# Windows of edges packed over groups of sixteen tiles in place of eight

## The chip, the cores and the metric

The kernel runs on one core of a Trainium2 chip. Its time is the time on the device, in microseconds, and the time of a version is the median of its runs. The core has five engines with instruction streams of their own: PE (TensorE, matrix products; PEld is its loading of weights), DVE (VectorE), ACT (ScalarE), POOL (GpSimd) and SP (SyncE). They meet at semaphores only. Transfers run on 16 DMA engines; the gathers of this kernel are issued by GpSimd.

## The reference

There are 50,000 nodes with 128 features and 100,000 directed edges: 25,000 random pairs, each in both directions, and one loop for each node, sorted by their end `dst`. Cut to what matters (`sage` three times, then one layer of attention):

```
h = relu(layernorm(x))
for l in range(3):                       # Wl, Wr, b of layer l
    agg = segment_sum(h[src], dst) / max(deg, 1)
    h = leaky_relu(agg @ Wl.T + b + h @ Wr.T, 0.01)
x = x + h
h = relu(layernorm(x)) @ W
e = leaky_relu(h[src] @ att_src + h[dst] @ att_dst, 0.2)
e = exp(e - segment_max(e, dst)[dst])
alpha = e / (segment_sum(e, dst)[dst] + 1e-16)
out = x + segment_sum(h[src] * alpha[:, None], dst) + bias
```

## The kernel before

**Tiles and passes.** The nodes are cut into 196 tiles of 256 (`NG`, `TILE`), each of two halves of 128. The program has a preparation and four passes over the tiles: passes 1 to 3 are the three layers (the third also does the sum with x, the second norm and `h @ W`), pass 4 is the attention. In a pass every engine goes through the tiles in one written order, `steps`, and at step t it works on tile t, or on one some steps behind.

**Windows.** The sums over edges are matrix products. A window is a list of up to 128 edges: `idx` has a column with their sources and `dcol` one with their ends. GpSimd gathers the 128 source rows of a window from the node table by one indirect DMA (L635), into one of 27 slots of `rows`. VectorE compares a row of numbers with the column of `dcol`, which gives a mask of 128 edges x 256 nodes (L1247; in pass 4 a bf16 form, L1249). TensorE multiplies rows by mask (L852, three matmuls a tile). Loops are not in the windows, a tile adds its own rows by itself.

**Lists.** A half tile has about 128 edges, some more and some fewer, so edges are packed over a group of `WG` = 8 tiles: its list has `GW` = 2 x 8 + 1 = 17 windows for 16 halves. Window k takes what half k - 1 has left over, and then edges of half k; the last takes only what is left. So a tile touches three windows, and shares two of them with its neighbours, except at the border of a group. The first tile of a group issues three gathers and each other one two (`s.new` in the code). There are 25 groups, and the last one has four tiles and 9 windows: 24 x 17 + 9 = 417 windows a pass. At the border the first and the last window of a group concern one half only, and `columns` gives their masks 128 columns in place of 256.

**Surplus.** `lead` is what a half finds left over from the halves before it in its group; it must not pass 128 at any window. If it does, `flag` is 0 and all engines take a general branch, which goes through the edges in 782 blocks of 128, each with an indirect load and an indirect store.

**How the surplus is found.** The preparation runs on 98 partitions (`HALF`), one for two tiles; a group of 8 tiles is `GROUP_ROWS` = 4 partitions. Each partition works out its surplus as if none came in, its total, and writes them to `carry`. TensorE moves `carry` down by 1, 2 and 3 partitions (L823, with the shifted unit matrices of `shift_m`, which GpSimd makes at L558). VectorE copies the result to `prev` and goes from the furthest partition to the nearest, three operations for each (L1110 to L1112); `later` (L1012) is 1 where the partition k before belongs to the same group. The helper `op` makes each operation of VectorE here wait for the one before it. Further on, the columns of `idx` and `dcol` are copied from PSUM, one copy for each partition of a group (L1178), and one for the last window of the groups (L1180).

**What lies around it.** Between these pieces VectorE does the statistics of the first norm for the 49 blocks of four tiles (`groups(a, b)`, L1034 to L1048), and ScalarE the norm itself (L662, L669). The node table is stored when the norm is done; the gathers of pass 1 wait for that.

**What orders a pass.** GpSimd issues gathers in order; before those of tile t it waits for the products of tile t - 12 to be done (`agg_done`, in pass 4 `pv_done`). TensorE waits at tile t for the masks and rows of it. In pass 4 ScalarE adds a score to each mask (L782), TensorE turns it (L953), VectorE takes the maximum (L1450).

Of the kernel before, what the change touches and what calls it, by code (L numbers as in the profile page):

```python
# [7 lines left out]
ALU = mybir.AluOpType  # L8
# [13 lines left out]
SG = 4  # L22
NSG = NG // SG
SW = 2 * SG + 1
WG = 8
GW = 2 * WG + 1
GROUPS = -(-NG // WG)
LAST_W = 2 * (NG - (GROUPS - 1) * WG) + 1
NWIN = (GROUPS - 1) * GW + LAST_W
GROUP_ROWS = WG // 2  # L30
RUN = 5 * P
# [8 lines left out]
HALF = NG // 2  # L40
# [22 lines left out]
class Step:  # L63


    def __init__(self, i, off):
# [12 lines left out]
        self.k = off % SG  # L79
        self.m = off % WG  # L80
        own = off // WG * GW + 2 * self.m
        self.w = own if i is None else WRING * i + own
# [86 lines left out]
def build(nc, x, src, dst, wl1, bl1, wr1, wlh, blh, wrh, w_gat, att_s, att_d, bias, out):  # L169
# [11 lines left out]
    with ctx:  # L181
        def sb(name, shape, dt=F32):
            return ctx.enter_context(nc.sbuf_tensor(name, shape, dt))
# [87 lines left out]
        nth_i = sb("nth_i", [HALF, 1], I32)  # L271
        later = sb("later", [HALF, GROUP_ROWS])
        came = sb("came", [HALF, 2])
        prev = sb("prev", [HALF, 9])
        carry = sb("carry", [HALF, 3])
        shift_m = sb("shift_m", [HALF, GROUP_ROWS - 1, HALF])
        stat = sb("stat", [P, 8])
# [79 lines left out]
        bank = [ctx.enter_context(nc.psum_tensor(f"bank{i}", [P, 512], F32)) for i in range(8)]  # L357
# [627 lines left out]
        def vector_program(eng):  # L985
# [9 lines left out]
            def op(ins):  # L995

                seq[0] += 1
                ins.then_inc(S["prep_seq"], 1)
                eng.wait_ge(S["prep_seq"], seq[0])
# [103 lines left out]
                                        ALU.mult, ALU.add))  # L1103
            op(eng.tensor_tensor(word[:, :, :], w_a[:, :, :], valid[:, :, :], ALU.mult))
            eng.wait_ge(S["chain_ps"], 1)
            op(eng.tensor_copy(prev[:, :], bank[1][0:HALF, 3:12]))
            op(eng.tensor_tensor(came[:, 0:1], prev[:, 6:7], later[:, 3:4], ALU.mult))
            for k in (2, 1):
                to = came[:, 0:1] if k > 1 else lead[:, 0:1]
                op(eng.tensor_tensor(came[:, 1:2], prev[:, 3 * k - 2:3 * k - 1], came[:, 0:1], ALU.add))  # L1110
                op(eng.tensor_tensor(came[:, 1:2], came[:, 1:2], prev[:, 3 * k - 3:3 * k - 2], ALU.max))
                op(eng.tensor_tensor(to, came[:, 1:2], later[:, k:k + 1], ALU.mult))  # L1112
# [685 lines left out]
        block.scalar(scalar_program)  # L1798
        block.tensor(tensor_program)
        block.vector(vector_program)  # L1800

_INS = ['x', 'src', 'dst', 'L0_gnn_Wl1', 'L0_gnn_bl1', 'L0_gnn_Wr1', 'L0_gnn_Wlh', 'L0_gnn_blh', 'L0_gnn_Wrh',
# [18 lines left out]
```

## Time and profile before

| | |
|---|---|
| median of 3 runs | 2512.96 us (2511.53 to 2515.49) |
| span of the profiled execution | 2514.0 us (its own time is not listed beside its span) |
| busy PE, DVE, ACT, POOL | 74%, 79%, 55%, 66% |
| gathers by L635 | 1251 in passes 1 to 3, 417 in pass 4 |
| DMA | 582.84 MB, 232 GB/s in the mean |
| preparation, to the first gather | 232.86 us |

The profile is one execution. A share of busy time is a mean over stages with different limits, so the stages are read apart: by the busy time in a stretch of time, by the rows of single instructions, and by the waits. The time in brackets at an instruction is the idle time of its engine before it and what ended it; "issue" means that nothing in the profile did.

### The profile page before, as it was taken

The page shows a single profiled execution, that of the slowest core. Times are in us where ns is not written, and L with a number is a line of the kernel's source. Part 1 is how long each engine was busy: PE and PEld are TensorE (multiplying, and loading weights), DVE is VectorE, ACT ScalarE, POOL GpSimd, SP SyncE. Part 2 cuts the span into 40 slices and gives each one's busy share as a digit, 9 for nine tenths or more (in the row PEclk, how much of TensorE's full clock was granted, in tenths as well). Part 3 has the DMA queues.
Part 4 walks back from the last instruction along what each step waited for, and adds up shares of the span by engine and source line. Part 5 has one row for each costly group of instructions (what it writes and reads, how often), then busy time and mean ns, then how long its engine had stood idle before and what let it go on. Part 6 is the DMA issues. An engine that isn't in the chain of part 4 may idle for free. (4 is left out here: it accounts for less than half of the span.)

```text
span 2514.0 us, 49419 instructions
## 1 busy us (share of the span) xinstructions
PE 1865.3 (74%) x12376; PEld 1627.8 (65%) x12376; DVE 1991.2 (79%) x8222; ACT 1393.8 (55%) x3711; POOL 1648.2 (66%) x1706
## 2 busy tenths in 40 slices
PE   0000888888886887888887999999999566666666
PEld 0000777777775777777766888888888456555555
DVE  7988766666664666666656999999999699999999
ACT  3696344444442222222223666666666688888887
POOL 2002777777775777777766777767672577777774
PEclk9999999999998999999998999999999799999998
DMA  6685788888886888888886988888888588887887
GB/s 207 216 296 204 235 249 245 247 249 246 249 248 180 244 253 244 244 251 242 251 231 200 264 263 261 258 256 255 257 256 234 139 205 204 206 202 202 205 203 174
DMA packets 597881, 582.84 MB, mean 232 GB/s; under 512 B 79531, under 2 KB 557349, under 8 KB 597568
## 3 DMA queue, kind: packets, MB, share of 16 engines
q1 hardware_dynamic: 402272, 337.58, 44.7%
q0 software_dynamic: 54208, 112.76, 21.0%
q10 hardware_dynamic: 141120, 129.32, 15.0%
q8 instruction: 107, 1.75, 0.3%
q14 instruction: 174, 1.43, 0.2%
HBM read 372.40 MB, written 207.75 MB: 231 GB/s over the span
## 5 line engine op out<-in xcount | busy, mean ns | idle before, releaser
L635 POOL DMA_INDIRECT rows<-tab,idx x1251 | 1229.4, 983 | 548.7 <-issue 342.6
L852 PE MATMUL bank<-mask,rows 128*128 128x128 f32 (+1 forms) x3528 | 645.6, 320 | 208.9 <-DMA rows<-tab,idx 185.9
L852 PEld LDWEIGHTS bank<-mask,rows 128*128 128x128 f32 x3528 | 543.9, 195 | 286.4 <-issue 165.6
L1267 DVE TENSOR_TENSOR sage<-bank,sage 128x256 f32<-128x256 f32 x588 | 247.2, 420 | 413.2 <-PE bank L852 410.9
L722 ACT ACTIVATE sage<-bank,b_col 128x256 f32<-128x256 f32 x392 | 185.9, 474 | 599.6 <-PE bank L878 599.1
L635 POOL DMA_INDIRECT rows<-tab_c,idx x417 | 398.1, 955 | 181.5 <-issue 115.8
L1247 DVE TENSOR_SCALAR mask<-iota,dcol 128x256 f32<-128x256 f32 (+1 forms) x1251 | 418.8, 365 | 0.1
L953 PE MATMUL bank<-ident,mask 128*128 128x128 f32 x784 | 139.9, 305 | 177.5 <-ACT mask L782 176.8
L1273 DVE TENSOR_TENSOR sage<-sage 128x256 f32<-128x256 f32 x588 | 246.3, 419 | 1.8 <-DMA sage<-inv_d 1.6
L1278 DVE SCALAR_TENSOR_TENSOR sage<-sage 128x256 f32<-128x256 f32 x588 | 243.0, 413 | 4.6 <-ACT sage L722 4.6
L877 PE MATMUL bank<-sage,wcat 128*128 128x256 f32 x784 | 236.9, 384 | 0.0
L878 PE MATMUL bank<-sage,wcat 128*128 128x256 f32 x784 | 236.0, 383 | 0.0
L953 PEld LDWEIGHTS bank<-ident,mask 128*128 128x128 f32 x784 | 90.8, 151 | 208.1 <-ACT mask L782 195.2
L963 PE MATMUL bank<-rows,sage 128*128 128x131 f32 x1568 | 224.3, 290 | 1.4 <-ACT sage L802 1.4
L782 ACT ACTIVATE mask<-cut_w,rows 128x256 f32<-128x256 bf16 (+1 forms) x417 | 181.0, 484 | 61.1 <-issue 39.0
L963 PEld LDWEIGHTS bank<-rows,sage 128*128 128x128 f32 x1568 | 207.6, 205 | 1.6 <-ACT sage L802 1.6
L691 ACT ACTIVATE sage<-sage,nmr,rstd 128x128 f32<-128x128 f32 x392 | 172.2, 486 | 42.9 <-DVE nmr L1224 41.6
L802 ACT ACTIVATE sage<-cut_w,ed 128x256 f32<-128x256 bf16 (+1 forms) x441 | 184.4, 473 | 4.9 <-DVE ed L1475 2.6
L917 PE MATMUL bank<-wcat,sage 128*128 128x128 f32 x784 | 177.3, 308 | 0.0
L886 PEld LDWEIGHTS bank<-ident,sage 128*128 128x128 f32 x784 | 152.9, 196 | 22.8 <-issue 4.9
L878 PEld LDWEIGHTS bank<-sage,wcat 128*128 128x128 f32 x784 | 150.9, 192 | 20.9
L1450 DVE TENSOR_REDUCE mx<-bank 128x2 f32<-128x512 f32 x196 | 132.7, 677 | 33.8 <-PE bank L953 33.4
(219 smaller groups left out, 3276.9 us busy)
## 6 DMA issues: line engine op xcount, KB each, us to landing
sage<-inv_d SPq DMA_DIRECT2D x588, 128.0 KB
turned<-sage ACTq DMA_DIRECT2D x392, 128.0 KB
tab<-sage ACTq DMA_DIRECT2D x392, 128.0 KB
sage<-turned SPq DMA_DIRECT2D x392, 128.0 KB
tab_c<-sage ACTq DMA_DIRECT2D x196, 132.0 KB
own_w<-tab_c SPq DMA_DIRECT2D x196, 132.0 KB, 2.9
tab<-sage SPq DMA_DIRECT2D x49, 512.0 KB, 3.5
xin<-tab SPq DMA_DIRECT2D x196, 128.0 KB
```

The costliest lines, as they stand in the source:

```text
L635: eng.indirect_dma_start(out=rows[:, s.win[w], 0:width], out_offset=None, in_=table, in_offset=bass.IndirectOffsetOnAxis(ap=idx[:, s.w + w ...
L722: eng.activation(new_t[:, o.v, :], ps_zz[ph][o.t % len(ps_zz[ph])][:, 0:TILE], ACT.Identity, bias=b_col[:, ph - 1:ph]).then_inc(S["z_a"], 1)
L802: m = eng.activation(prob[:, o.mw[w], a:b], cut[:, o.win[w], a:b], ACT.Exp, bias=ed[:, o.g, 2 * o.k + w:2 * o.k + w + 1])
L852: m = eng.matmul(to[:, a:b], rows[:, s.win[w], 0:D], mask[:, s.mw[w], c:c + b - a], start=(w == 1), stop=(w == 2))
L877: eng.matmul(to, wcat[:, ph - 1, D:2 * D], own_t[:, o.v, :], start=True, stop=False)
L878: eng.matmul(to, wcat[:, ph - 1, 0:D], agg_t[:, o.r, :], start=False, stop=True).then_inc(S["dense_done"], 1)
L953: m = eng.transpose(ps_z[s.t % 3][:, j * TILE + n * P:j * TILE + (n + 1) * P], score[:, s.mw[j + n], (1 - n) * P:(2 - n) * P], ident[:, :])
L963: m = eng.matmul(ps_o[o.k][:, j * TILE:j * TILE + D + 3], prob[:, o.mw[j + n], (1 - n) * P:(2 - n) * P], rows[:, o.win[j + n], 0:D + 3], s ...
L1247: m = eng.tensor_scalar(to[:, g.mw[w], a:b], io[:, a:b], node, None, ALU.is_equal)
L1267: eng.tensor_tensor(agg_t[:, o.r, :], ps[:, 0:TILE], own_t[:, o.v, :], ALU.add).then_inc(S["sum_v"], 1)
L1273: eng.tensor_tensor(agg_t[:, o.r, :], agg_t[:, o.r, :], inv_b[:, o.r, :], ALU.mult).then_inc(S["t_v"], 1)
L1278: eng.scalar_tensor_tensor(at, at, 0.01, at, ALU.mult, ALU.max).then_inc(S["l_v"], 1)
```

## The change

`WG` becomes 16. A group is then 16 tiles or 8 partitions, a list 33 windows for 32 halves, and there are 13 groups, the last one again with four tiles and 9 windows: 12 x 33 + 9 = 405 windows. The surplus is carried over 32 halves, and a partition takes it from the seven before it. `GW`, `GROUPS`, `LAST_W`, `NWIN`, `GROUP_ROWS` and the sizes of `later` and `shift_m` follow from `WG`. Behind the new line all line numbers are higher by one.

```diff
--- before.py
+++ after.py
@@ -22,7 +22,7 @@
 SG = 4
 NSG = NG // SG
 SW = 2 * SG + 1
-WG = 8
+WG = 16
 GW = 2 * WG + 1
 GROUPS = -(-NG // WG)
 LAST_W = 2 * (NG - (GROUPS - 1) * WG) + 1
@@ -271,7 +271,7 @@
         nth_i = sb("nth_i", [HALF, 1], I32)
         later = sb("later", [HALF, GROUP_ROWS])
         came = sb("came", [HALF, 2])
-        prev = sb("prev", [HALF, 9])
+        prev = sb("prev", [HALF, 3 * (GROUP_ROWS - 1)])
         carry = sb("carry", [HALF, 3])
         shift_m = sb("shift_m", [HALF, GROUP_ROWS - 1, HALF])
         stat = sb("stat", [P, 8])
@@ -1103,9 +1103,10 @@
                                         ALU.mult, ALU.add))
             op(eng.tensor_tensor(word[:, :, :], w_a[:, :, :], valid[:, :, :], ALU.mult))
             eng.wait_ge(S["chain_ps"], 1)
-            op(eng.tensor_copy(prev[:, :], bank[1][0:HALF, 3:12]))
-            op(eng.tensor_tensor(came[:, 0:1], prev[:, 6:7], later[:, 3:4], ALU.mult))
-            for k in (2, 1):
+            op(eng.tensor_copy(prev[:, :], bank[1][0:HALF, 3:3 * GROUP_ROWS]))
+            far = GROUP_ROWS - 1
+            op(eng.tensor_tensor(came[:, 0:1], prev[:, 3 * far - 3:3 * far - 2], later[:, far:far + 1], ALU.mult))
+            for k in range(far - 1, 0, -1):
                 to = came[:, 0:1] if k > 1 else lead[:, 0:1]
                 op(eng.tensor_tensor(came[:, 1:2], prev[:, 3 * k - 2:3 * k - 1], came[:, 0:1], ALU.add))
                 op(eng.tensor_tensor(came[:, 1:2], came[:, 1:2], prev[:, 3 * k - 3:3 * k - 2], ALU.max))
```

On VectorE, in the preparation, where the surplus of the partitions before is added up (before, then after; `came` is the surplus that comes in):

```order
L1106 COPY prev<-bank 98x9
L1107 TENSOR_TENSOR came<-prev,later 98x1
L1110 TENSOR_TENSOR came<-prev,came 98x1
L1111 TENSOR_TENSOR came<-came,prev 98x1
L1112 TENSOR_TENSOR came<-came,later 98x1
L1110 TENSOR_TENSOR came<-prev,came 98x1
L1111 TENSOR_TENSOR came<-came,prev 98x1
L1112 TENSOR_TENSOR lead<-came,later 98x1
```

```order
L1106 COPY prev<-bank 98x21
L1108 TENSOR_TENSOR came<-prev,later 98x1
L1111 TENSOR_TENSOR came<-prev,came 98x1
L1112 TENSOR_TENSOR came<-came,prev 98x1
L1113 TENSOR_TENSOR came<-came,later 98x1
```

The last three rows stand six times in a row now, the last time with `lead` as what is written. So there are 12 more operations between the copy of `prev` and the windows' places.

On GpSimd, the gathers of passes 1 to 3 and of pass 4 (as a difference):

```order
 L606 ISA x2
 L607 COMPARE_AND_BRANCH
-L635 DMA rows<-tab,idx 128x128 x1251
-L635 DMA rows<-tab_c,idx 128x132 x417
+L635 DMA rows<-tab,idx 128x128 x1215
+L635 DMA rows<-tab_c,idx 128x132 x405
 L607 UNCONDITIONAL_BRANCH
```

There are 36 gathers fewer in the first three passes and 12 in the fourth. The copies of L1178 into `idx` and `dcol`, four each before, of 96 or 100 columns, are eight each now, of 48 or 52 columns.

On VectorE in pass 1, at the border behind the eighth tile (before, then after; `mask` is what the window's comparison writes):

```order
L1247 TENSOR_SCALAR mask<-iota,dcol 128x256
L1247 TENSOR_SCALAR mask<-iota,dcol 128x128
L1273 TENSOR_TENSOR sage<-sage 128x256
L1267 TENSOR_TENSOR sage<-bank,sage 128x256
L1247 TENSOR_SCALAR mask<-iota,dcol 128x128
L1247 TENSOR_SCALAR mask<-iota,dcol 128x256 x2
```

```order
L1248 TENSOR_SCALAR mask<-iota,dcol 128x256 x2
L1274 TENSOR_TENSOR sage<-sage 128x256
L1279 SCALAR_TENSOR_TENSOR sage<-sage 128x256
L1268 TENSOR_TENSOR sage<-bank,sage 128x256
L1248 TENSOR_SCALAR mask<-iota,dcol 128x256 x2
```

The two half masks, one at the end of a group and one at the start of the next, have become one whole mask that both tiles share.

## Rows read from the trace of the kernel before

**Rows 1.** Busy time (instructions) of PE, PEld, DVE, ACT, POOL; clock, DMA share, GB/s.

```profile
161.00:229.00 68.00, 0.00 (x0) 0.00 (x0) 52.70 (x348) 68.00 (x188) 0.00 (x0) 1.00 0.82 285
233.00:768.00 535.00, 449.90 (x2690) 397.47 (x2691) 345.79 (x1013) 219.30 (x572) 408.12 (x417) 1.00 0.82 239
785.00:1313.00 528.00, 422.49 (x2300) 369.22 (x2301) 325.11 (x985) 141.56 (x376) 400.88 (x417) 0.96 0.84 242
1400.00:1900.00 500.00, 497.70 (x3350) 423.34 (x3348) 486.69 (x2091) 317.41 (x958) 358.35 (x354) 1.00 0.89 258
1990.00:2490.00 500.00, 328.72 (x2985) 296.55 (x2986) 482.92 (x2452) 440.59 (x1051) 379.01 (x398) 0.94 0.81 201
```

**Rows 2.** Timeline of POOL: start, duration, instruction [idle before].

```profile
232.86 1.00 POOL L635 DMA_INDIRECT rows<-tab,idx  x1 [100.06 <-DMA tab<-sage]
...
767.29 0.94 POOL L635 DMA_INDIRECT rows<-tab,idx  x1 [0.30 <-issue]
785.04 0.94 POOL L635 DMA_INDIRECT rows<-tab,idx  x1 [16.81 <-DMA tab<-sage]
...
1311.76 0.94 POOL L635 DMA_INDIRECT rows<-tab,idx  x1 [0.30 <-issue]
...
1965.61 0.94 POOL L635 DMA_INDIRECT rows<-tab_c,idx  x1 [54.76 <-DMA tab_c<-sage]
...
2489.55 0.94 POOL L635 DMA_INDIRECT rows<-tab_c,idx  x1 [0.30 <-issue]
```

**Rows 3.** Waits of POOL in passes 3 and 4: us, times, longest.

```profile
POOL rows L635 <- PE bank L852: 58.5, 90, 0.9
...
POOL rows L635 <- PE bank L963: 11.0, 36, 0.3
```

**Rows 4.** Waits of PE in passes 1 and 2, of DVE in 1990:2490.

```profile
PE bank L852 <- DMA rows<-tab,idx: 62.4, 79, 1.9
...
PE bank L852 <- DMA rows<-tab,idx: 107.4, 97, 10.7
...
DVE mx L1450 <- PE bank L953: 11.3, 19, 1.7
```

**Rows 5.** Groups by form: count | busy, mean ns of one | idle before.

```profile
L635 POOL DMA_INDIRECT rows<-tab,idx x1251 | 1229.4, 983 | 548.7 <-issue 342.6 <-DMA tab<-sage 134.1 <-PE bank L852 71.9
...
L635 POOL DMA_INDIRECT rows<-tab_c,idx x417 | 398.1, 955 | 181.5 <-issue 115.8 <-DMA tab_c<-sage 54.8 <-PE bank L963 11.0
L1247 DVE TENSOR_SCALAR mask<-iota,dcol 128x256 f32<-128x256 f32 x1101 | 383.5, 375 | 0.0
...
L1249 DVE TENSOR_SCALAR cut_w<-iota_b,dcol 128x256 bf16<-128x256 bf16 x367 | 94.6, 290 | 0.0
L1247 DVE TENSOR_SCALAR mask<-iota,dcol 128x128 f32<-128x128 f32 x150 | 44.3, 295 | 0.1
...
L1249 DVE TENSOR_SCALAR cut_w<-iota_b,dcol 128x128 bf16<-128x128 bf16 x50 | 15.1, 303 | 0.0
```

**Rows 6.** Timeline of DVE and ACT in the preparation.

```profile
73.06 0.16 DVE L1110 TENSOR_TENSOR came<-prev,came 98x1 f32<-98x1 f32 x1
...
74.03 0.16 DVE L1112 TENSOR_TENSOR lead<-came,later 98x1 f32<-98x1 f32 x1
...
154.89 1.14 DVE L1178 TENSOR_SCALAR idx<-bank 128x100 int32<-128x100 f32 x4
156.06 0.20 DVE L1180 TENSOR_SCALAR idx<-bank 128x24 int32<-128x24 f32 x1
...
160.82 0.30 ACT L662 ACTIVATE std<-mv,eps 128x8 f32<-128x8 f32 x1 [0.84 <-DVE mv L1039]
```

**Rows 7.** Waits in the preparation; a DMA issue: count, us to landing.

```profile
POOL row_d L579 <- DVEq L1027: 5.1, 1, 5.1
...
PE bank L826 <- DVEq L1125: 11.0, 1, 11.0
...
head<-packed,slice_i POOLq DMA_INDIRECT x5, 3.5
```

## The prediction

> **What bounds the kernel now.** I read the cut into stages first, then the issue rows of GpSimd's gathers, then who waits for whom in each stage. The program has a preparation (0 to 233 us) and four passes over the 196 tiles. [rows 1] give, for each pass, the busy time of the engines, and no engine looks full in passes 1 and 2: TensorE is busy 449.9 of 535 us and 422.5 of 528 us, VectorE less, GpSimd 408.1 and 400.9. In the steady part of pass 3 TensorE is busy 497.7 of 500 us. In pass 4 VectorE is busy 482.9 of 500 us and GpSimd 379.0.
>
> Busy time misleads for GpSimd. [rows 2] are its issue rows: a gather takes 0.94 us, and 0.30 us of idle time stand before the next, put down to "issue". So a gather costs 1.25 us, and 0.94 of it counts as busy. By the starts of the first and last of 417, pass 1 issues them from 232.86 to 767.29 us (1.285 us each, some slow ones at its start among them), pass 2 from 785.04 to 1311.76 (1.266), pass 4 from 1965.61 to 2489.55 (1.259). [rows 3] say that in pass 4 GpSimd never waits for a free buffer: the longest wait on TensorE is 0.3 us, which is the gap that is there anyway (36 cases; passes 1 and 2 have the same row with 23 and 21). In pass 3 it is otherwise: 90 waits, 58.5 us, the longest 0.9; there GpSimd is held back. The other side agrees. [rows 4]: in passes 1 and 2 TensorE waits 79 and 97 times for gathered rows (62.4 and 107.4 us), and in the steady part of pass 3 it is full [rows 1]. So passes 1 and 2 are paced by the number of gathers, pass 3 by TensorE, and pass 4 by gathers with VectorE close behind: there VectorE waits 19 times for scores from TensorE, 11.3 us in all in 500.
>
> The preparation is a chain on two engines. ScalarE waits for VectorE a last time before 160.82 us [rows 6]; from 161 to 229 us it is busy 68.00 of 68 us [rows 1], and the first gather follows at 232.86 [rows 2].
>
> **The change part by part.**
>
> *Gathers.* A list of windows now covers 16 tiles with 33 windows in place of 2 x 17 = 34. With 13 lists in place of 25 there are 12 x 33 + 9 = 405 windows in place of 417: 12 gathers fewer in each pass, 1215 and 405 in place of the counts of [rows 5].
> - Passes 1 and 2: 12 x 1.266 = 15.2 us each, by the mean of pass 2, since the slow gathers at the start of pass 1 stay. The next limit in these passes is TensorE: 422.5 busy of 528, so a pass of 513 us leaves it 90 idle. DMA engines are busy 0.84 of pass 2 at 242 GB/s, and 0.89 at 258 GB/s in pass 3 [rows 1], so the denser traffic has been carried. Bounds: 9 to 16 us for each.
> - Pass 3: TensorE's matmuls are the same in number and shape (three for each tile), and it is full. 0 us, at most the 2.6 us that VectorE saves there.
> - Pass 4: 12 x 1.259 = 15.1 us if GpSimd alone decides. But VectorE is nearly as late: 482.9 busy of 500. What it can give back is the 11.3 us that it waits for scores [rows 4] and its own saving of 3.8 us (below), together 15.1, and to get all of it no gap could be left. At the low end only the 3.8 comes. I take 12 us, nearer to the upper end, since the waits are there now and late rows are what makes them.
>
> *Masks.* At each of the 12 list borders that go, two half masks (128 columns) become one whole mask (256). Pass by pass on VectorE: 2 x 295 - 375 = 215 ns, 12 times: 2.6 us; in pass 4 with the bf16 form, 2 x 303 - 290 = 316 ns, 12 times: 3.8 us [rows 5]. In passes 1 and 2 this lies beside VectorE's waits for TensorE and is worth nothing. ScalarE's score activations shrink in the same way in pass 4, where it is not the bound (440.6 of 500).
>
> *Carrying the surplus over seven rows.* Here the change adds. Each operation of the preparation waits for the one before it, so an operation costs the distance of two starts: from 73.06 to 74.03 us there are five, 0.195 us each [rows 6].
> - Four more comparisons for `later`: 0.8 us, ahead of the load of `row_d`, for which GpSimd waits 5.1 us on VectorE [rows 7]; they shift that load.
> - Four more turns of three operations: 12 x 0.195 = 2.3 us.
> - The copies into `idx` and `dcol`: eight of 48 or 52 columns for four of 96 or 100, twice. Four of 100 columns take 154.89 to 156.06 us, 0.29 each with the gaps; one of 24 columns takes 0.20, and 0.03 of gap [rows 6]. So 0.25 each: 8 x 0.25 - 1.17 = 0.84, twice 1.7 us.
> - Four small matmuls on TensorE and four selects on GpSimd: behind the three matmuls of before TensorE waits 11.0 us for VectorE, and behind its selects GpSimd waits the 5.1 us [rows 7]. Both cost nothing; without that cover they would be about a microsecond.
>
> Sum: 4.8 us on VectorE. Behind these operations stand the statistics of the next tiles, and ScalarE waits for those. Its 0.84 us of idle time at 160.82 us is a wait for VectorE, so nothing absorbs the delay, and it moves all that follows. Bounds: 3 us (the `later` part hidden by DMA) to 6 us.
>
> *Sum.* Against the profiled span of 2514.0 us: + 4.8 - 15.2 - 15.2 - 0 - 12 = -37.6, that is 2476.4. The span stands 1.0 us above the median of the runs, 2512.96, so the median should come to 2475.4 us. I say 2475.
>
> **Weighed against the skill.** The page Perfetto Trace Analysis of the Trainium skill, section Identifying the Most-Contended Engine, says that for Vector, Scalar and GpSimd occupancy names the bottleneck. By that rule TensorE limits passes 1 and 2 and VectorE pass 4, the gathers are worth nothing, and the time would be that of rival B. The trace speaks against it: the 0.30 us between gathers is not counted as occupancy, yet it is there in every one [rows 2]. The page SBUF — State Buffer of the Trainium skill, section A bandwidth-pool intuition that's wrong, says that HBM is almost always the end-to-end bottleneck. By that the saving is by bytes, which is rival C.
>
> **The rivals.**
> - A. Pass 4 is VectorE's. Its 482.9 of 500 us speak for it, its 19 waits for scores against. Then pass 4 gives 3.8 us in place of 12: 2475.4 + 8.2 = 2483.6.
> - B. Something paid per tile sets the pace of passes 1, 2 and 4 (TensorE at 450 of 535 us, VectorE in pass 4). Only VectorE's 3.8 us come, and the preparation costs 4.8: 2514.0. Against it: TensorE's 176 waits for gathered rows.
> - C. The DMA engines set the pace (0.82, 0.84 and 0.81 busy). Twelve gathers are 12 x 64 KB = 0.79 MB: at 239 and 242 GB/s 3.3 and 3.2 us, in pass 4 0.81 MB at 201 GB/s 4.0 us. 2512.96 + 4.8 - 10.5 = 2507.3. Against it: gathers leave at an even 1.25 us, and pass 3 carries 258 GB/s.
> - D. Slower: the surplus runs over. A window takes 128 edges, and what is left of one half tile must fit into the next window; if a surplus passes 128 anywhere, the flag falls and the program takes its general branch. A surplus now adds up over 31 halves of tiles, not 15. I counted it from the inputs that the reference draws: a half tile has 128 edges in the mean with a deviation of 12.9, the largest surplus is 82 with lists of 8 tiles and 112 with 16. It decides from 129 on, and 16 edges are left. Price, an estimate: 4 passes x 782 blocks, each with three DMAs in a chain, at 3.5 us to landing as for `head` [rows 7], over 32,000 us.
>
> **How the numbers follow.** Forecast 0.70, A 0.18, B 0.03, C 0.05, D 0.01, and 0.03 for what I don't see. The forecast's own ends: passes 1 and 2 together 26 to 31 us, pass 4 from 8 to 15, preparation 6 to 3, pass 3 0 to 1: from 2512.96 - 28 = 2485 to 2512.96 - 44 = 2469. With A, and somewhat less in passes 1 and 2 beside it, the range is 2468 to 2487, which leaves out B, C, D and some of the tails. A measurement of this kernel can tell about 0.2% from no change, 5 us. Faster by more than that (below 2507.9): forecast, A, most of C and of the unseen: 0.94. Within it: B and part of C: 0.04. Slower: D and a rest, 0.02.
>
> **What would show it right or wrong.** Gathers 1215 and 405 at an unchanged 0.94 + 0.30 us; the first of them at 237.7 us in place of 232.86; from the first start to the last 519, 512 and 512 us in passes 1, 2 and 4, and pass 3 as long as before. VectorE's waits for scores in pass 4 fall from 11.3 us to 2 or less, and its share nears 0.98. It is wrong if a gather's gap grows, if passes 1 and 2 shrink by 3 us rather than 15, if the first gather still comes at 233 us, or if pass 4 keeps 520 us.

## The result, and the profile after

The changed kernel takes 2477.19 us, the median of 4 runs (2476.73 to 2483.16), and the kernel before, run beside it, 2514.22 (4 runs, 2511.53 to 2517.24). The ratio is 0.9861, with a 95% interval of 0.9849 to 0.9872. The prediction was 2475 us.

The profiled execution of the changed kernel has a span of 2481.4 us. It is the slowest of its four runs: the spans of the others are 2475.0, 2475.1 and 2475.8. So the two traces differ by 32.6 us, and the medians by 37.0.

Busy time by stage after the change, with the columns of [rows 1]:

```profile
161.00:229.00 68.00, 0.00 (x0) 0.00 (x0) 53.27 (x371) 65.80 (x182) 0.00 (x0) 1.00 0.81 288
238.00:757.00 519.00, 449.77 (x2691) 398.55 (x2692) 344.55 (x1000) 220.12 (x572) 395.54 (x405) 1.00 0.83 245
774.00:1286.00 512.00, 416.02 (x2295) 365.44 (x2296) 323.97 (x971) 141.37 (x376) 388.77 (x405) 0.97 0.85 247
1373.00:1873.00 500.00, 497.65 (x3321) 420.01 (x3320) 485.96 (x2066) 314.58 (x949) 344.43 (x339) 1.00 0.87 255
1963.00:2457.00 494.00, 329.19 (x3000) 294.54 (x3000) 481.47 (x2448) 441.95 (x1045) 373.02 (x389) 0.95 0.79 202
```

The timeline of GpSimd, at the first and last gather of each pass, as in [rows 2]:

```profile
238.25 2.29 POOL L635 DMA_INDIRECT rows<-tab,idx  x1 [101.87 <-DMA tab<-sage]
...
756.31 0.95 POOL L635 DMA_INDIRECT rows<-tab,idx  x1 [0.30 <-issue]
774.07 0.95 POOL L635 DMA_INDIRECT rows<-tab,idx  x1 [16.81 <-DMA tab<-sage]
...
1285.46 0.98 POOL L635 DMA_INDIRECT rows<-tab,idx  x1 [0.31 <-issue]
1303.22 1.08 POOL L635 DMA_INDIRECT rows<-tab,idx  x1 [16.78 <-DMA tab<-sage]
...
1887.43 0.96 POOL L635 DMA_INDIRECT rows<-tab,idx  x1 [0.30 <-issue]
1944.26 0.94 POOL L635 DMA_INDIRECT rows<-tab_c,idx  x1 [55.87 <-DMA tab_c<-sage]
...
2457.40 0.94 POOL L635 DMA_INDIRECT rows<-tab_c,idx  x1 [0.30 <-issue]
```

From these starts and those of before, the whole difference can be laid out. Pass 3 of before runs from 1329.98 to 1909.89 us by the same view.

| stage | before, us | after, us | difference | predicted |
|---|---|---|---|---|
| up to the first gather | 232.86 | 238.25 | +5.4 | +4.8 |
| pass 1, first start to last | 534.43 | 518.06 | -16.4 | -15.2 |
| pass 2 | 526.72 | 511.39 | -15.3 | -15.2 |
| pass 3 | 579.91 | 584.21 | +4.3 | 0 |
| pass 4 | 523.94 | 513.14 | -10.8 | -12 |
| between the passes and at the end | 116.1 | 116.3 | +0.2 | 0 |

Passes 1 and 2 are as long as their gathers: 518.06 / 404 = 1.282 us and 511.39 / 404 = 1.266 us a gather, the 1.285 and 1.266 of before, with 12 fewer. The engines' busy times hardly moved (TensorE 449.90 to 449.77 us in pass 1, 422.49 to 416.02 in pass 2), their idle time went. Two things are not as predicted. Pass 3 is longer, and in pass 4 the waits did not go away.

The waits in the stretches of [rows 3] and [rows 4]; first GpSimd in the whole of pass 3 (1303 to 1888 us), then GpSimd and VectorE in pass 4 (1963 to 2457), then TensorE in passes 1 and 2; columns us, times, longest:

```profile
POOL rows L635 <- PE bank L852: 92.4, 135, 1.2
...
POOL rows L635 <- PE bank L963: 17.0, 47, 1.4
...
DVE mx L1451 <- PE bank L953: 9.2, 16, 1.2
...
PE bank L852 <- DMA rows<-tab,idx: 45.4, 70, 2.0
...
PE bank L852 <- DMA rows<-tab,idx: 98.8, 98, 10.7
```

In pass 3 GpSimd is held back more than before (92.4 us for 58.5), as it has fewer gathers to issue in a pass that did not get shorter. In pass 4 it is now held up now and then: its longest wait for TensorE was 0.3 us and is 1.4. TensorE still waits for gathered rows in passes 1 and 2. The groups by form show the counts that were to come, 1215 and 405, and whole masks in place of halves, as in [rows 5]:

```profile
L635 POOL DMA_INDIRECT rows<-tab,idx x1215 | 1194.0, 983 | 558.0 <-issue 310.3 <-DMA tab<-sage 135.5 <-PE bank L852 112.2
L635 POOL DMA_INDIRECT rows<-tab_c,idx x405 | 388.2, 959 | 181.7 <-issue 108.8 <-DMA tab_c<-sage 55.9 <-PE bank L963 17.0
...
L1248 DVE TENSOR_SCALAR mask<-iota,dcol 128x256 f32<-128x256 f32 x1137 | 397.4, 377 | 0.0
...
L1248 DVE TENSOR_SCALAR mask<-iota,dcol 128x128 f32<-128x128 f32 x78 | 22.5, 288 | 0.1
```

Last, the preparation. Four places on VectorE's timeline and one on ScalarE's, to be laid beside [rows 6]:

```profile
74.39 0.16 DVE L1111 TENSOR_TENSOR came<-prev,came 98x1 f32<-98x1 f32 x1
...
77.69 0.16 DVE L1113 TENSOR_TENSOR lead<-came,later 98x1 f32<-98x1 f32 x1
...
158.24 1.90 DVE L1179 TENSOR_SCALAR idx<-bank 128x52 int32<-128x52 f32 x8
160.17 0.18 DVE L1181 TENSOR_SCALAR idx<-bank 128x12 int32<-128x12 f32 x1
...
165.66 0.30 ACT L662 ACTIVATE std<-mv,eps 128x8 f32<-128x8 f32 x1 [2.20 <-DVE mv L1039]
```

The turns (the three operations for each partition) begin 1.33 us later than before (74.39 for 73.06) and end 3.66 later (77.69 for 74.03). The copies begin 3.35 later, and `idx` and `dcol` take 1.93 us each to the start of the short one in place of 1.17. ScalarE's last wait for VectorE ends 4.84 us later (165.66 for 160.82) and has grown from 0.84 to 2.20 us.

One more place belongs here, near the start: the last memset of GpSimd and an operation of VectorE (L1005), before and after:

```profile
7.24 0.32 POOL L568 MEMSET mask<- 128x264 f32 x1
...
7.10 0.53 DVE L1005 TENSOR_SCALAR first<-ones,d_nat 125x128 f32<-125x128 f32 x1 [3.90 <-DMA d_nat<-in_dst]
```

```profile
8.44 0.33 POOL L568 MEMSET mask<- 128x264 f32 x1
...
6.84 2.00 DVE L1005 TENSOR_SCALAR first<-ones,d_nat 125x128 f32<-125x128 f32 x1 [3.64 <-DMA d_nat<-in_dst]
```

GpSimd ends 1.2 us later, after its seven selects and a larger memset of `shift_m`. VectorE's operation ends less than 0.1 us behind it in both kernels, and took 2.00 us in place of 0.53.

### The profile page after: what moved, and what is told of

It is laid out like the page before. It is cut to its first block and busy times, and to the rows that moved or that the text cites. A ratio compares the mean times of both kernels' runs of the same rounds, so it can differ in the third digit from the quotient of the medians.

```text
span 2481.4 us, 49369 instructions
## 1 busy us (share of the span) xinstructions
PE 1863.2 (75%) x12384; PEld 1624.2 (65%) x12384; DVE 1993.1 (80%) x8196; ACT 1393.1 (56%) x3699; POOL 1604.0 (65%) x1662
## 3 DMA queue, kind: packets, MB, share of 16 engines
q10 hardware_dynamic: 141120, 129.32, 15.2%
## 5 line engine op out<-in xcount | busy, mean ns | idle before, releaser
L635 POOL DMA_INDIRECT rows<-tab,idx x1215 | 1194.0, 983 | 558.0 <-issue 310.3
L635 POOL DMA_INDIRECT rows<-tab_c,idx x405 | 388.2, 959 | 181.7 <-issue 108.8
L691 ACT ACTIVATE sage<-sage,nmr,rstd 128x128 f32<-128x128 f32 x392 | 172.2, 486 | 43.1 <-DVE nmr L1225 43.1
L684 ACT ACTIVATE std<-mv,eps 128x2 f32<-128x2 f32 x196 | 58.0, 296 | 181.1 <-DVE mv L1213 181.0
```

The source lines that it names most:

```text
L635: eng.indirect_dma_start(out=rows[:, s.win[w], 0:width], out_offset=None, in_=table, in_offset=bass.IndirectOffsetOnAxis(ap=idx[:, s.w + w ...
```

## Experiments

Only the last two (e11_short_add_again and e12_lists32) ran on a core like the first one (the kernel before takes 2519.41 us there). The other ten ran on cores where the kernel before takes 2926.60, 2921.03 and 2887.28 us; there a comparison is made only with the kernel before on the same core, or between runs on one of them. Most expectations give their microseconds for a core like the first; on the others these are not put to the test, only the theories and rivals are. The edits named "left out" skip gathers: the slot then keeps the rows of an earlier gather, and masks, matmuls and all else stay.

The lengths of the passes on those cores, from the first start of a gather to the last, in us (mean per gather). The first three rows are of the core with 2926.60 us, e8_scan of that with 2921.03, the last two of that with 2887.28:

| run | first gather at | pass 1 | pass 2 | pass 3 | pass 4 |
|---|---|---|---|---|---|
| e1_prep_only, 417 gathers | 238.39 | 630.76 (1.516) | 616.95 (1.483) | 648.36 (1.559) | 650.05 (1.563) |
| e2_out12, 405 | 234.16 | 612.03 (1.515) | 601.75 (1.490) | 631.16 (1.562) | 631.10 (1.562) |
| e4_out49, 368 | 233.35 | 561.11 (1.529) | 548.57 (1.495) | 594.12 (1.619) | 593.88 (1.618) |
| e8_scan, 405 | 231.93 | 613.58 (1.519) | 599.04 (1.483) | 631.35 (1.563) | 625.66 (1.549) |
| e9_changed, 405 | 238.06 | 605.77 (1.499) | 593.48 (1.469) | 621.04 (1.537) | 618.60 (1.531) |
| e10_lists24, 401 | 231.83 | 600.14 (1.500) | 587.49 (1.469) | 614.92 (1.537) | 613.56 (1.534) |

### Preparation alone

The kernel before, with the operations that the change adds, on data of their own that nothing uses, and each copy into `idx` and `dcol` made in two:

```diff
+            for k in range(4):
+                op(eng.tensor_scalar(more[:, k:k + 1], later[:, 0:1], float(k), None, ALU.is_ge))
...
+            for k in range(4):
+                op(eng.tensor_tensor(more[:, 1:2], prev[:, 0:1], more[:, 0:1], ALU.add))
+                op(eng.tensor_tensor(more[:, 1:2], more[:, 1:2], prev[:, 1:2], ALU.max))
+                op(eng.tensor_tensor(more[:, 0:1], more[:, 1:2], later[:, 1:2], ALU.mult))
...
+                    for a, b in ((0, 12), (12, n)):
```

> The kernel before with its lists of 8 tiles, and only the work that the change adds to the preparation of VectorE: four more comparisons behind later, four more turns of three operations (on a tile that nothing reads), and the copies into idx and dcol cut in two each. Theory (all of it lies on the path to the first gather): the first gather comes 5 us later (238 us in place of 232.9) and the whole takes 5 us more, about 2519. Rival (the wait for DMA and the slack of ScalarE hide it): first gather and time as before.

Measured: 2930.05 us, 1.0011 of before (1.0001 to 1.0021), that is 3.45 us more by the medians. The timeline of GpSimd in this run, its first gather, and the first and last of pass 2:

```profile
238.39 1.06 POOL L636 DMA_INDIRECT rows<-tab,idx  x1 [102.89 <-DMA tab<-sage]
...
902.88 0.94 POOL L636 DMA_INDIRECT rows<-tab,idx  x1 [32.78 <-DMA tab<-sage]
...
1519.83 0.94 POOL L636 DMA_INDIRECT rows<-tab,idx  x1 [0.30 <-issue]
```

The first gather is at 238.39 us, where e2_out12, e3_out12_p4 and e4_out49 of the same core, with the preparation of before, have it at 234.16, 234.44 and 233.35. So VectorE's added operations delay the first gather by 4 to 5 us, as counted, and the whole by about as much. The added matmuls of TensorE and selects of GpSimd are not in this run.

### Gathers alone

The kernel before, with 12 gathers of each pass left out (`return w == 0 and t % 16 == 8`), the same in pass 4 only, and 49 of each pass left out (`return w == 1 and t % 4 == 2`):

```diff
+def left_out(t, w, ph):
+    return w == 0 and t % 16 == 8
...
-                    for w in s.new:
+                    for w in issued(s.t, ph):
```

> The kernel before without the first gather of every second list (12 gathers in each pass; the masks, waits and all other work stay, and the rows of an older window are used in their place). Theory (the number of gathers paces passes 1, 2 and 4): each of passes 1 and 2 is 15 us shorter from first to last gather, pass 4 by 10 or 11, pass 3 unchanged: 2514 - 41 = 2473. Rival C (bytes): 3 us for each of passes 1, 2 and 4, about 2505. Rival B (work per tile): 2514.

> The kernel before without the first gather of every second list in pass 4 alone (12 gathers). VectorE's masks are as before. Theory (GpSimd first, VectorE close behind it): 8 to 11 us less, about 2504. If GpSimd alone paces pass 4: 15 us less, 2499. If VectorE does (rival A): no change, since its work is untouched.

> The kernel before without 49 gathers in each pass (one in every fourth tile). Shows where the next limit stands. Theory: passes 1 and 2 still go by the gathers, 368 x 1.266 = 466 us each, 61 less; pass 3 stays at 580; pass 4 stops at VectorE, whose busy time is 0.966 of it, at 506 to 510 us, some 16 less: 2514 - 61 - 61 - 16 = 2376. If gathers pace pass 4 too, it takes 463 us and the whole 2330. If TensorE stops passes 1 and 2, they stay above 480 us.

> The kernel before without 49 gathers in each pass (one in every fourth tile), once more, since the core of the first set takes 2927 us for the kernel before in place of 2514. On a core like that of the profile: passes 1 and 2 at 466 us each (61 less), pass 3 at 580, pass 4 at 506 to 510 because VectorE stops it, all in all 2376. If gathers alone pace pass 4 too, it takes 463 us and the whole 2330. If TensorE stops passes 1 and 2, they stay above 480 us.

Measured: e2_out12 2855.48 us, 0.9752 (0.9736 to 0.9769), -71.1 us; e3_out12_p4 2909.20, 0.9939 (0.9922 to 0.9955), -17.4; e4_out49 2681.32, 0.9163 (0.9142 to 0.9184), -245.3; its second run on another core 2679.36, 0.9175 (0.9160 to 0.9190). GpSimd's first and last gather of pass 2 in e2_out12:

```profile
880.88 0.94 POOL L645 DMA_INDIRECT rows<-tab,idx  x1 [33.75 <-DMA tab<-sage]
...
1482.63 0.95 POOL L645 DMA_INDIRECT rows<-tab,idx  x1 [0.30 <-issue]
```

Per gather left out: 71.1 / 48 = 1.48 us, 17.4 / 12 = 1.45, 245.3 / 196 = 1.25. On those cores this decides two things. Nothing but gathers was taken away, so rival B (work per tile) is out: it gives nothing here. Twelve gathers are 0.79 MB, 3.3 us at the transfer rate of [rows 1], and 14 us in four passes; 71 came, so rival C (bytes) is out. In pass 4 alone 17.4 us came with VectorE's work unchanged. This does not speak against rival A on the first core: VectorE is busy 492.07 of 650 us in pass 4 of e1_prep_only, and 482.92 of 500 us in [rows 1]. With 49 fewer the mean rises to 1.62 us in passes 3 and 4; that other engines begin to count there is read from the mean and was not tested. With 12 left out of a pass, each gave 1.45 to 1.48 us, more than the 1.25 from start to start; what makes up the rest was not found. No run left gathers out on a core like the first one. There the evidence is the changed kernel itself, whose passes 1 and 2 became shorter by the price of 12 gathers.

Pass 3 also shrank there, by 17.2 us (648.36 to 631.16), where the prediction gave it nothing.

### The changed kernel and its preparation

The changed kernel with the carry made by one product, one scan and one copy in place of 19 operations, the comparisons for `later` moved behind the first statistics, and three copies each into `idx` and `dcol` in place of nine:

```diff
-            for k in range(far - 1, 0, -1):
...
+            op(eng.tensor_tensor_scan(sofar[:, :], live[:, ::-1, 1], live[:, ::-1, 0], 0.0, ALU.add, ALU.max))
...
-                for o in range(GROUP_ROWS):
...
+                op(eng.tensor_scalar(view[:, 0:full, 0:GW - 1].rearrange("p g (o k) -> p g o k", k=4), whole, less, None,
```

> The changed kernel with a cheaper preparation: the surplus of the seven partitions by one product and one scan in place of 19 operations, the comparisons for later moved behind the first statistics into a wait for DMA, and the copies into idx and dcol three each in place of ten each. Same result. Theory (all of VectorE's work here is on the path): 16 operations of 0.195 us less, 0.8 to 1.6 us from later, and 2 x 1.3 us from the copies: 6 to 7 us less than the changed kernel, 2470 on a core where that takes 2477, first gather at 232 us or before. Rival: hidden, no change.

> The changed kernel as it is, beside the kernel before, on whatever core this set gets. On a core like that of the profile (2514 us before): 2477, ratio 0.985. On the core of the first two sets, where the kernel before takes 2921 to 2927 us and TensorE lags behind its gathers: leaving 12 gathers a pass out gave 71 us there, and the preparation costs 3 to 5: about 2856, ratio 0.977.

> Lists of 24 tiles (9 lists, 49 windows each, 401 windows in all) with the cheap preparation of e8_scan; the surplus is taken from eleven partitions. The largest surplus that I count from the inputs is 126, so the fast branch must still be taken. Same result. Theory: 16 gathers a pass fewer than the kernel before and 4 fewer than the changed one: 5 us for each of passes 1, 2 and 4 beyond e8_scan, and a preparation of the length of e8_scan's, so some 20 us less than the changed kernel, 2457 on a core where that takes 2477. Rival: pass 4 stops at VectorE and gives nothing further, 2462.

Measured: e8_scan 2850.29 us, 0.9755 (0.9739 to 0.9772) of before on its core; e9_changed, the changed kernel itself, 2826.54, 0.9789 (0.9776 to 0.9803) on another. With the scan and lists of 24 tiles (`WG = 24`, 401 gathers) e10_lists24 takes 2797.71 us, 0.9687 (0.9674 to 0.9700). GpSimd's first gather in e8_scan:

```profile
231.93 2.55 POOL L638 DMA_INDIRECT rows<-tab,idx  x1 [99.59 <-DMA tab<-sage]
```

It comes at 231.93 us. On the same core e6_short_add and e7_no_gathers_p3, which have the preparation of the changed kernel, have it at 239.53 and 238.19, and e5_out49_again, with the preparation of before, at 234.54. So the whole cost of the preparation can be had back, and 2.6 us more. e10_lists24 beats both kernels: 28.8 us less than the changed kernel on the same core. In the traces it is 27.8 us: 6.2 in the preparation (238.06 to 231.83) and 22.8 in the four passes for 4 x 4 = 16 gathers, 1.4 us each, while the pauses are 1.2 us longer.

### Who sets the pace of pass 3

Two experiments on the changed kernel. One shortens an addition of VectorE in pass 3 from 2 x 128 columns to 2 x 8, so that part of x1b is left out. The other leaves out all gathers of pass 3 (`return ph == 3`).

```diff
-                    eng.tensor_tensor(x1b[:, b.b, :, :], x1[:, b.r, :, :],
-                                      b_bc[:, LAYERS, :].unsqueeze(1).to_broadcast([P, 2, D]), ALU.add
+                    eng.tensor_tensor(x1b[:, b.b, :, 0:8], x1[:, b.r, :, 0:8],
+                                      b_bc[:, LAYERS, 0:8].unsqueeze(1).to_broadcast([P, 2, 8]), ALU.add
```

> The changed kernel with the addition of the bias in pass 3 (VectorE, 0.40 us a tile) over 8 of 128 columns, so the residual stream is not what the reference has; all other work stays. Theory formed after the result (VectorE paces pass 3: its masks became 14 ns longer in the mean and the tile 28 ns, two masks a tile): pass 3 falls from 3.17 us a tile to TensorE's limit, by at most 0.25 us a tile, some 30 to 50 us in all. Rival (the prediction's: TensorE paces pass 3, busy 99.5%): no change.

> The changed kernel with no gathers in pass 3 (the products use the rows left from pass 2). Theory (a mask that starts while GpSimd is in a certain part of a gather takes 500 ns in place of 335, and VectorE paces pass 3): all masks of pass 3 take about 335 ns, 65 ns less in the mean, two a tile: 0.13 us a tile, some 26 us less. Rival (TensorE paces pass 3): the masks get shorter and the pass does not.

Measured: e6_short_add 2856.33 us, 0.9771 (0.9754 to 0.9788); e7_no_gathers_p3 2779.60, 0.9517 (0.9502 to 0.9533). On the same core e8_scan is 0.9755; it is the changed kernel with the cheaper preparation. Busy time in 1600 to 2080 us (the steady part of pass 3; columns as in [rows 1]) of e8_scan, e6_short_add and e7_no_gathers_p3, in this order:

```profile
1600.00:2080.00 480.00, 449.07 (x3099) 385.47 (x3098) 442.73 (x1926) 286.31 (x887) 309.00 (x305) 1.00 0.86 246
```

```profile
1600.00:2080.00 480.00, 450.97 (x3113) 389.76 (x3112) 416.44 (x1936) 286.45 (x890) 309.49 (x306) 0.99 0.87 247
```

```profile
1600.00:2080.00 480.00, 479.60 (x3326) 420.25 (x3325) 465.51 (x2066) 314.67 (x951) 0.00 (x0) 1.00 0.75 219
```

VectorE is idle 37 of 480 us on that core, and taking more of its work away brings next to nothing: it does 26 us less, and pass 3 lasts 629.39 us from first gather to last in place of 631.35. Without gathers the core gets through 7% more instructions of TensorE in the same time (3326 for 3099). From the last gather of pass 2 to the first of pass 4 it then needs 639.2 us in place of 713.9 (e6_short_add), so half of the gain lies in the slow start of the pass, which goes away with the gathers. With the gathers gone VectorE is busy 97% there, as on the first core. So on that core the gathers, and what waits for them, hold pass 3 back, and the experiment says nothing on the first core, where VectorE is idle 14 of 500 us and TensorE 2. The addition was therefore tried again, and the core was one like the first:

> The changed kernel with the add of x1b in pass 3 made over 8 of its 128 columns, so part of the output's computation is left out: 0.4 us less VectorE work in every tile of pass 3, and nothing else. It is run a second time for a core like the first, where VectorE was busy 485.96 of 500 us in pass 3 and the longer masks were seen. Theory (VectorE, with masks of 335 or 500 ns, sets the pace of pass 3 there): pass 3 falls from 3.17 us a tile to 3.10 or less, where TensorE's own 497.65 of 500 us would hold it, so 8 to 15 us less in pass 3, and nothing elsewhere. Rival (TensorE sets the pace, as the prediction said): pass 3 stays within 2 us of what the changed kernel takes on the same kind of core. On a core like those of the other experiments both say nothing new: 0.977 of the kernel before, pass 3 at 3.24 us a tile.

Measured: 2432.39 us (before 2519.41), 0.9655 (0.9639 to 0.9671), where the changed kernel had 0.9861 beside its own kernel before. In the traces, 2431.7 against 2481.4 us: pass 3 lasts 541.07 us in place of 584.21, the pause behind it 52.1 in place of 56.8, and passes 1, 2 and 4 differ by 519.38 - 518.06, 509.87 - 511.39 and 510.85 - 513.14, under 2.3 us each. The steady part of pass 3 in this run:

```profile
1373.00:1823.00 450.00, 449.87 (x3243) 402.61 (x3243) 435.77 (x2017) 307.18 (x927) 329.30 (x335) 1.00 0.93 277
```

Two of VectorE's groups by form in that stretch (count | busy, mean ns | idle before), of the changed kernel and then of this one:

```profile
L1248 DVE TENSOR_SCALAR mask<-iota,dcol 128x256 f32<-128x256 f32 x306 | 123.8, 405 | 0.0
...
L1355 DVE TENSOR_TENSOR sage<-sage,b_bc 128x256 f32<-128x256 f32 x159 | 63.6, 400 | 0.0
```

```profile
L1248 DVE TENSOR_SCALAR mask<-iota,dcol 128x256 f32<-128x256 f32 x299 | 107.5, 360 | 0.0
...
L1355 DVE TENSOR_TENSOR sage<-sage,b_bc 128x16 f32<-128x16 f32 x154 | 23.6, 153 | 0.2 <-DMA x_d<-sage 0.2
```

The addition became 0.247 us shorter a tile (400 to 153 ns). From one start of it to the next, in these stretches, a tile went from 3.164 to 2.916 us, and VectorE's busy time in it from 3.075 to 2.823; over the whole pass it is 43.1 us / 196 = 0.22 us a tile. VectorE sets the pace of pass 3 on that core, nearly one to one, and is still 97% busy. The other half is as important: TensorE was "full" before, 497.65 of 500 us, and it is full now, 449.87 of 450, with 7.2 instructions in a microsecond in place of 6.6. The expectation allowed pass 3 at most 15 us, since "TensorE's own 497.65 of 500 us would hold it"; it gave 43. A busy share of TensorE near one is no proof that it is the bound; its instructions in a microsecond tell more.

### Lists over 32 tiles

One number of the changed kernel (`WG = 32`); the surplus then reaches 151 edges.

> The changed kernel with lists over 32 tiles: counted from the inputs the largest surplus is then 151, over the 128 of a window. By rival D the flag falls and the program takes its general branch: 4 passes of 782 blocks with three dependent DMAs each, over 32,000 us. If the branch were cheaper than the estimate (its DMAs overlapping), some 10,000 us. If the surplus decided nothing, 2,800 us or less.

Measured: 63,992.85 us, one run. GpSimd's longest waits (us, times, longest):

```profile
POOL se L1549 <- DMA gen_s<-mask: 15286.1, 4, 5730.2
POOL gen_s L1559 <- DVE mask L1693: 8548.6, 2346, 4.3
POOL mask L1554 <- DMA se<-edges: 8111.6, 3124, 2.7
```

The program is in its general branch, where for each of 3128 blocks small loads, gathers and a store wait on one another. Rival D's mechanism is real, and its price is twice the 32,000 us that the prediction gave as the least: 64.0 ms / 3128 blocks is 20.5 us a block. It decides between 24 and 32 tiles with these inputs (surplus 126 and 151).

## Why the prediction was right, and where not

- **Gathers, not busy engines, set passes 1 and 2: right.** Predicted 15.2 us each, measured 16.4 and 15.3. The gap of 0.30 us stayed, and so did 1.266 us a gather in pass 2. Of the 1.2 us more in pass 1, 1.0 is that its mean gather fell from 1.2847 to 1.2823 us. e11_short_add_again, which is the changed kernel in these passes, has 519.38 and 509.87 us. The experiments with nothing but gathers left out show the cause by itself, but on the other kind of core and at another price.
- **Preparation: right in size, 4.8 for 5.4 us, with one step wrong.** By places: the turns 2.33 us (predicted 2.3), the copies 2 x 0.76 = 1.5 (1.7), and what lies ahead of the turns 1.33 (0.8). The step that failed there is that the four selects on GpSimd cost nothing, since GpSimd waits 5.1 us for VectorE behind them. VectorE itself was held up: its operation L1005 ended 1.2 us later, right behind GpSimd's last memset. In all thirteen traces of the fast branch it ends 77 to 80 ns after that memset, and takes 0.53 to 2.81 us; in e1_prep_only, without the selects, it ends as early as before (7.64 us; before 7.63, after 8.84). No run changed GpSimd's work alone, so this is read from the ends. With the comparisons for `later` (0.75 us as counted) the operations ahead of `row_d` came 2.03 us late, and 1.33 of it reached the turns. Another 0.3 us was lost again ahead of the copies. ScalarE's last wait and its last operation both end 4.84 us late, as summed. The other 0.55 us arise behind ScalarE: from there to the first gather it is 3.42 us before and 3.97 after, while the last rows of the node table are stored. Why this takes longer was not found.
- **Pass 4: right in size, 12 for 10.8 us, wrong in what the profile was to show.** VectorE's waits for scores were to fall from 11.3 us to 2 or less; they are 9.2 us in 494, and VectorE's share is 0.975, from 0.966. What took the rest of the 15.1 us is on GpSimd: its mean per gather rose from 1.259 to 1.270 us, 4.3 us in all, and its waits for TensorE from 11.0 to 17.0 us. That both engines hold the pass, by turns, is an inference from these rows. Rival A would have shown 3.8 us; here it was 10.8, and 13.1 in e11_short_add_again (510.85 us), which also shows how far two executions differ in this pass.
- **Pass 3: the step "pass 3 by TensorE" failed.** The prediction costed it at 0 because TensorE is busy 497.7 of 500 us. Its value was nearly right and its reason wrong. TensorE did 3321 instructions in 500 us, and 3243 in 450 once VectorE had less to do, so e11_short_add_again shows that VectorE sets the pace there on this kind of core. With VectorE as the bound, the 2.6 us of masks should have come, and pass 3 became 4.3 us longer instead. The trace shows what took their place: the 256-wide masks of pass 3 went from 395 to 405 ns in the mean (next section), so that masks cost 0.82 us a tile as before ((118.5 + 11.7)/159 and (123.8 + 5.4)/158). Busy time of VectorE per tile rose from 3.054 to 3.075 us, which over 196 tiles is 4 us. Where all of it arises was not settled, and part may belong to this one execution, the slowest of four.
- **Rivals.** B (2514.0 us) and C (2507.3) are refuted by the result, 2477.19 us, and their mechanisms by the runs with gathers left out, on the other kind of core. D's point, a surplus over 128, is confirmed from its far side, and its price was 64,000 us, twice the estimate. The surplus of 112 stayed under 128, and the program took its fast branch.
- **The rule of the most-contended engine, misread.** The prediction takes it that by this rule TensorE limits passes 1 and 2. But the same section of the page Perfetto Trace Analysis of the Trainium skill says not to judge TensorE by the busy time of its matmuls, and to take its share of the peak rate and its weight loads instead. Against the weight loads (397.47 and 369.22 us in [rows 1]) GpSimd is the busiest engine in both passes, with 408.12 and 400.88 us, and the rule names what the result names. The 497.65 of 500 us of pass 3 were a busy time of matmuls, and e11_short_add_again bears the section out. What the busy time of GpSimd does not show is that it is at its limit at 76% (408.12 of 535 us).

The sum: the terms missed by +0.6, -1.2, -0.1, +4.3 and +1.2 us in the traces, +5.0 with the pauses, and the median by 2.2, within the range of 2468 to 2487. That it came so near is in part luck: pass 3 had its value for a wrong reason, and the selects of GpSimd and the 0.55 us behind ScalarE, neither of them in the sum, were partly made up for by waits ahead of the turns and the copies. The other three executions, with spans of 2475.0 to 2475.8 us for the predicted 2476.4, have no trace, so how their parts differ is open.

## What to carry to other kernels

For a queue of gathers, count starts: the distance from start to start is the price, and the idle time "issue" between two of them belongs to it. Before counting an operation as hidden behind a wait, look at what the engine that is waited for was itself held up by. An engine that shows 99% busy may be paced by one at 97%; shorten one operation of the other and see whether the full one really holds. When lists are packed more densely, find out from the data how near the fallback is: four gathers a pass more were to be had at 24 tiles, and at 32 the time was 26 times as long.

## What the runs showed of the hardware

**Masks and gathers.** In pass 3 a mask of VectorE takes 0.33 or 0.50 us. VectorE in a piece of pass 3 after the change, and GpSimd in the same piece:

```profile
1601.76 0.48 DVE L1248 TENSOR_SCALAR mask<-iota,dcol 128x256 f32<-128x256 f32 x1
...
1602.89 0.33 DVE L1248 TENSOR_SCALAR mask<-iota,dcol 128x256 f32<-128x256 f32 x1
...
1604.92 0.50 DVE L1248 TENSOR_SCALAR mask<-iota,dcol 128x256 f32<-128x256 f32 x1
```

```profile
1601.02 1.11 POOL L635 DMA_INDIRECT rows<-tab,idx  x1 [0.75 <-PE bank L852]
1602.43 0.95 POOL L635 DMA_INDIRECT rows<-tab,idx  x1 [0.30 <-issue]
1604.13 1.17 POOL L635 DMA_INDIRECT rows<-tab,idx  x1 [0.75 <-PE bank L852]
```

The long ones start 0.74 and 0.79 us after the start of a gather, the short one 0.46 us. Over 1373 to 1873 us, 103 masks that start 0.7 to 0.8 us in take 497 ns in the mean, and 123 that start 0.4 to 0.5 us in take 330. Additions and products of 256 columns keep 0.40 to 0.42 us in the mean at every distance. Distance alone does not decide: 22 masks at 0.5 to 0.6 us take 508 ns, and in pass 3 of e8_scan and e9_changed, on the other cores, 37 and 54 masks at 0.7 to 0.8 us take 341 and 342. Of the 103 long ones 100 stand beside a gather that had been held up, with over 0.4 us of idle time before it; of the 91 short ones just named only 2 do. In e11_short_add_again, with the addition shortened, 12% of the masks of pass 3 took over 0.43 us (44 of 363) in place of 39% (141 of 362). So what a change in pass 3 is worth depends also on how masks and gathers fall together.

That gathers lengthen the masks is read from the two timelines. The run without gathers in pass 3 agrees, but tests little: none of its 367 masks takes over 355 ns, yet with gathers on the same core only 2 of 363 (e6_short_add) and 5 of 365 (e8_scan) take over 430. The Trainium skill, page SBUF — State Buffer, section SBUF: two separate sides, says that VectorE and GpSimd share a pair of ports under an exclusive lock, for some kinds of VectorE's operations. The end of L1005 right behind GpSimd's memset agrees with such a lock, and so may the masks. The additions, with two inputs in SBUF, are a kind that the section counts in as well where GpSimd's operation reads SBUF, and they were not lengthened here. The section does not say what a gather holds, and for how long.

**Other cores.** The same program took 2887 to 2927 us in three sets of runs and 2513 to 2519 us in the other two. Whether this belongs to the core is not shown: the record gives chip 6 both for a set with 2926.60 us and for the one with 2519.41, without saying whether it is one chip. A gather takes 0.94 to 0.95 us on both, but GpSimd waits longer at starts of tiles. Its waits in pass 2 (us, times, longest), of the kernel before on the first core and then of e1_prep_only:

```profile
POOL rows L635 <- issue: 120.4, 395, 0.3
...
POOL rows L635 <- PE bank L852: 6.4, 21, 0.3
```

```profile
POOL rows L636 <- remote: 68.5, 36, 6.0
POOL rows L636 <- PE bank L853: 35.2, 26, 2.0
```

Busy time in pass 2 of e1_prep_only, with the columns of [rows 1]:

```profile
903.00:1520.00 617.00, 438.37 (x2192) 368.16 (x2193) 299.30 (x943) 139.39 (x358) 401.40 (x417) 0.87 0.69 198
```

GpSimd's busy time is that of [rows 1] (400.88 us), and the granted clock of TensorE is lower, 0.87 for 0.96. The clock alone does not explain it: in 1600 to 2080 us of e8_scan it is 1.00, and the pace is still 6.46 instructions of TensorE in a microsecond for 6.64 in the steady part on the first core. The pause between passes 1 and 2 is longer too, 33.7 us for 17.8. The change was worth more there, 0.9789 for 0.9861. Why these sets differ, and what stands behind "remote", was not found.
